# Two-layer paged attention: output products in threes over the next group, and every fourth head transposed by a DMA from ScalarE's queue

## The reference, cut to what matters

```python
x = x + einsum('bct,bcd->bdt', x, weights[subjects])      # x: (32, 32, 512) f32
q, k, v = x @ Wq.T, x @ Wk.T, x @ Wv.T                     # 32 query heads, 8 key heads, D = 128
q, k = rope(rmsnorm(q, q_norm_w), pos), rope(rmsnorm(k, k_norm_w), pos)
k_all = concatenate([k_cache[block_table], k])             # 16 pages of 32 keys, and 32 new keys
v_all = concatenate([v_cache[block_table], v])
scores = where(valid, q @ k_all.T * SCALE, -1e30)          # four query heads share a key head
o = softmax(scores) @ v_all                                # (b, 32, 32 heads * 128)
x = x + o @ Wo.T                                           # (32, 32, 512)
```

## Time and profile before

| | us |
|---|---|
| Median of three runs | 1043.12 |
| Profiled execution, its time | 1038.51 |
| Profiled execution, its span | 1036.7 |
| PE busy (8329 matmuls) | 977.4 (94%) |
| DVE busy | 795.4 (77%) |
| ACT busy | 713.1 (69%) |
| POOL busy | 495.6 (48%) |
| DMA, mean rate over the span | 286 GB/s |

### The profile page before, as it was taken

One profiled execution on the slowest core, in us unless ns is written; L12 is line 12 of the kernel. 1 busy time (PEld: TensorE's weight loads), 2 busy tenths in 40 slices (PEclk: granted clock), 3 DMA queues, 4 the chain that ended last, 5 costly groups with the idle time before them and its releaser, 6 DMA issues.

```text
span 1036.7 us, 24928 instructions
## 1 busy us (share of the span) xinstructions
PE 977.4 (94%) x8329; PEld 775.4 (75%) x8329; DVE 795.4 (77%) x1706; ACT 713.1 (69%) x1943; POOL 495.6 (48%) x642
## 2 busy tenths in 40 slices
PE   3889999999889999899999999999999999999998
PEld 2678888887678788668868857866976986895793
DVE  6789999999997788757857866865875884785680
ACT  4788999988765788647846755764864774675670
POOL 6455666566881266526424623632540641552340
PEclk9999999999999999999999999999999999999999
DMA  5789999989989899768998998997999999899840
GB/s 201 252 303 337 320 384 369 384 279 399 377 289 319 313 329 356 263 186 271 344 252 260 339 266 218 330 299 203 343 295 229 308 317 240 258 359 252 239 147 11
DMA packets 268017, 296.49 MB, mean 286 GB/s; under 512 B 94065, under 2 KB 225649, under 8 KB 265329
## 3 DMA queue, kind: packets, MB, share of 16 engines
q1 hardware_dynamic: 249200, 227.65, 71.7%
q0 software_dynamic: 18688, 67.25, 18.7%
HBM read 231.77 MB, written 46.27 MB: 268 GB/s over the span
## 4 chain that ended last, share of the span: by engine, by line
PE 56%; DVE 14%; SPq 8%; DMA 6%; issue 6%; ACT 6%; POOL 3%; ACTq 0%; DVEq 0%; POOLq 0%
PE ps_o L1410 16%; PE ps_proj L1410 16%; PE ps_o L1488 8%; SPq L641 5%; PE ps_s L1448 4%; PE ps_s L1452 4%; PE ps_t L1459 3%; DMA kt<-k_pages_t 3%; DVE probs L1150 2%; PE ps_rt L1558 2%; DMA vs<-v_pages,v_row 2%; DVE c_stage L1306 1%; PE ps_o L1502 1%; DVE rot L1278 1%; DVE pt L1170 1%
## 5 line engine op out<-in xcount | busy, mean ns | idle before, releaser
L868 POOL TENSOR_SCALAR probs<-probs,recip 128x544 f32<-128x544 f32 (+1 forms) x256 | 158.4, 619 | 376.9 <-DVE recip L1158 373.0
L933 ACT ACTIVATE probs<-probs,neg_max 128x544 f32<-128x544 f32 x256 | 191.3, 747 | 158.2 <-DVE neg_max L1150 157.5
L1150 DVE CUSTOM_DVE_ANT_0 probs<-ps_s,mask,row_scale 128x544 f32<-128x544 f32 x256 | 200.1, 782 | 121.2 <-PE ps_s L1452 118.7
L1488 PE MATMUL ps_o<-pt,vs 128*128 128x128 f16 x3072 | 213.0, 219 | 5.4 <-DVE result L1192 2.5
L1488 PEld LDWEIGHTS ps_o<-pt,vs 128*128 128x128 f16 x3072 | 191.1, 98 | 16.3 <-issue 6.6
L822 POOL TENSOR_TENSOR roped<-rot 128x256 f32<-128x256 f32 x160 | 143.8, 921 | 79.4 <-DVE rot L1270 76.9
L1410 PE MATMUL ps_proj<-wt_hi,x0t_hi 128*128 128x512 f32 x384 | 158.6, 413 | 8.7 <-DVE x0t_lo L1108 7.2
L1410 PE MATMUL ps_o<-wo,ot_hi 128*128 128x512 f16 x512 | 153.5, 382 | 10.0 <-DVE ot_lo L1182 10.0
L1410 PE MATMUL ps_proj<-wt_hi,x0t_lo 128*128 128x512 f32 x384 | 150.7, 392 | 0.0
L1410 PE MATMUL ps_proj<-wt_lo,x0t_hi 128*128 128x512 f32 x384 | 149.8, 390 | 0.0
L856 POOL DMA_INDIRECT vs<-v_pages,v_row x128 | 131.7, 1029 | 22.2 <-issue 19.7
(11 more groups left out here) (145 smaller groups left out, 1590.2 us busy)
## 6 DMA issues: line engine op xcount, KB each, us to landing
kt<-k_pages_t SPq DMA_DIRECT2D x512, 128.0 KB
c_nat<-in_L_cond_k_cache SPq DMA_DIRECT2D x32, 512.0 KB, 5.8
q_t<-stage SPq DMA_DIRECT2D x64, 256.0 KB, 7.5
c_nat<-in_L_cond_v_cache SPq DMA_DIRECT2D x32, 512.0 KB, 7.0
qt<-q_t SPq DMA_DIRECT2D x32, 512.0 KB, 5.6
w_nat<-in_L_cond_Wq SPq DMA_DIRECT2D x8, 1024.0 KB, 8.4
k_pages_t<-c_stage SPq DMA_DIRECT2D x16, 512.0 KB, 5.6
c_nat<-in_L_cond_Wo SPq DMA_DIRECT2D x16, 512.0 KB, 8.1
```

Of the source, the lines that this page charges most:

```text
L868: pool.tensor_scalar(part, part, col(recip, i), 1.0, ALU.mult, ALU.mult).then_inc(p_norm, 1)
L933: act.activation(pr, pr, ACT.Exp, bias=col(neg_max, i), scale=-1.0, accum_out=col(row_sum, i)).then_inc(a_exp, 1)
L1150: dve.tensor_tensor_reduce(out=probs_of(i), in0=ps_s[:, score_cols(i):score_cols(i) + KEYS], in1=mask[(i // HK) % 2][:, mask_at(i):mask_at ...
L1488: ins = pe.matmul(ps_o[n % 2][:, jl * P:(jl + 1) * P], v[:, part, :], pt[i % NPT][:, NCH * half + c, :], start=jl == 0 and c == 0 and k == ...
```

## The change

It has five parts.

1. The projection of a group has a bank of its own, `ps_y`. Its 32 heads of three products each are laid over steps -1 to 28 of the next group, nearly always one head a step (`Y_AT`); for the last group they follow in four steps (`Y_LAST`). `ps_t` has two banks in place of three; up to step 28 `ps_y` serves as the third. `add_residual` runs once per group.
2. So that contexts of the next group can be written while heads of this one are still being read, `ot_hi` and `ot_lo` change their layout from group to group: a head's 128 tokens lie 8 elements apart in even groups and 32 apart in odd ones. ACT and DVE read `ps_o` with a step of 64 or 32 elements to write them. Even groups keep their tokens in another order, which the residual's load and the store undo.
3. From step 52 on each fourth head (i % 4 == 3) is turned by DMA, 51 in all. ACT asks for it, at step i - 1 (`turn_rows`). SP's loop has only keys, queries, new values and results.
4. The new values are weighed in four products over 96 rows in place of eight over 128: `ptn` holds high, low and high again, the last copied by POOL (`tn_copy`). ACT and DVE write `ptn` in two instructions in place of one, and a step earlier. Three DMAs bring a `vn` instead of four, and it needs no zeroes.
5. Wo's late heads are split at two steps in five, up to step 48; one in four on POOL throughout.

```diff
-    vn = [sb(f"vn{i}", [4 * SEQ, HK // 2, 2, 2 * D], F16) for i in range(2)]
+    vn = [sb(f"vn{i}", [3 * SEQ, HK, D], F16) for i in range(2)]
...
-    ptn = [sb(f"ptn{i}", [4 * SEQ, 2, P], F16) for i in range(2)]
-    ot_hi = sb("ot_hi", [P, HQ, GB, SEQ], F16)
-    ot_lo = sb("ot_lo", [P, HQ, GB, SEQ], F16)
+    ptn = [sb(f"ptn{i}", [3 * SEQ, 2, 2, P], F16) for i in range(2)]
+    QUARTER = HQ // GB
+    ot_hi = sb("ot_hi", [P, HQ * GB * SEQ], F16)
+    ot_lo = sb("ot_lo", [P, HQ * GB * SEQ], F16)
     result = [sb(f"result{i}", [P, HID]) for i in range(2)]
     ps_s = psum("ps_s", [P, 3 * CH])
-    NTB = 3
+    NTB = 2
     ps_t = [psum(f"ps_t{i}", [P, CH]) for i in range(NTB)]
     ps_o = [psum(f"ps_o{i}", [P, HPC * P]) for i in range(2)]
+    ps_y = psum("ps_y", [P, HID])
...
-    STEPS = NP2 + 2 * HPC + 3
+    STEPS = NP2 + HPC
     GSTEPS = GB * HK
-    YPARTS = 8
-    YHEADS = HQ // YPARTS
-    YWIN = YPARTS // NHALF
     NBG = GB * NHALF
 
     def at(i, place):
@@ -432,13 +430,12 @@
         n, rest = divmod(i - place, HPC)
         return n if rest == 0 and 0 <= n < NHB else None
 
-    TN, TNE, OE = HPC - 1, HPC, HPC + 2
-    DMA_FIRST, DMA_LAST, STAGED = 2, 11, 3
+    TN, TNE, TNC, OE = HPC - 1, HPC - 1, HPC, HPC + 2
+    DMA_FIRST, STAGED, T_THIRD = 52, 3, 28
 
     def by_dma(i):
 
-        g, r = divmod(i, GSTEPS)
-        return 0 < i < NP2 and g >= 1 and (DMA_FIRST if g > 1 else 8) <= r <= DMA_LAST
+        return DMA_FIRST <= i < NP2 and i % HPC == HPC - 1
...
+    t_banks = [0]
+    for kind, i in tjobs[1:]:
+        t_banks.append((t_banks[-1] + 1) % (3 if (i if kind == "t" else HPC * i + TN) < T_THIRD else NTB))
+
+    def t_bank(kind, i):
+
+        return (*ps_t, ps_y)[t_banks[tjob_no[kind, i]]]
+
+    def held_by(n):
+
+        return max((m for m in range(n) if t_banks[m] == t_banks[n]), default=-1)
+
+    Y_AT = {r: (r + 1,) for r in range(-1, 3)} | {3: (4, 5), 4: (6, 7)} | {r: (r + 3,) for r in range(5, HQ - 3)}
+    Y_LAST = {-1: range(0, 4), 0: range(4, 10), 1: range(10, 16), 2: range(16, HQ)}
+    Y_OUT, Y_OUT_LAST = HQ - 3, 3
...
+    def y_heads(i):
+
+        g = y_group(i)
+        return (Y_AT if g + 1 < NG else Y_LAST).get(i - GSTEPS * (g + 1), ()) if g >= 0 else ()
...
+    def head_at(g, n):
+
+        if g % 2 == 1:
+            return n
+        k, j = divmod(n, QUARTER)
+        return HQ // NHALF * (k // NHALF) + NHALF * j + k % NHALF
+
+    def head_tokens(tile, g, n):
+
+        if g % 2 == 1:
+            return tile[:].rearrange("p (m h) -> p m h", h=HQ)[:, :, n]
+        k, j = divmod(n, QUARTER)
+        return tile[:].rearrange("p (k m j) -> p k m j", k=GB, j=QUARTER)[:, k, :, j]
...
     def late_head(i):
 
-        if i >= LATE_PAIRS:
-            n = WO_EARLY + LATE_PAIRS // 2 + i - LATE_PAIRS
-        else:
-            n = WO_EARLY + i // 2 if i % 2 == 1 else HQ
-        return n if 0 <= i and n < HQ else None
+        k, r = divmod(i, 5)
+        n = WO_EARLY + 2 * k + r // 2
+        return n if i >= 0 and r in (1, 3) and n < HQ else None
 
     def on_pool(n):
-        return n in range(*WO_POOL) and n % 4 == 3
+        return n >= WO_EARLY and n % 4 == 3
...
-        hh = HQ // NHALF
-        return tile[:, hh * h:hh * (h + 1), b % GB, :]
+        g, a = divmod(b, GB)
+        if g % 2 == 1:
+            return tile[:].rearrange("p (a t s h) -> p a s t h", a=GB, t=SEQ, s=NHALF)[:, a, h]
+        return tile[:].rearrange("p (s q a j) -> p s q a j", s=NHALF, a=GB, j=QUARTER)[:, h, :, a]
...
+    def context(n):
+
+        return ps_o[n % 2][:].rearrange("p (h t) -> p t h", t=SEQ if n // NBG % 2 == 1 else NHALF * SEQ)
...
-                for j in range(4):
-                    width = (2 - j // 2) * D
-                    sp.dma_start(vn[s][SEQ * j:SEQ * (j + 1), :, j % 2, 0:width],
-                                 v_new[b].rearrange("t (m j) f -> j t m f", j=2)[j % 2, :, :, 0:width]
-                                 ).then_inc(d_vn[s], 16)
+                for j in range(3):
+                    part = (0, 0, 1)[j]
+                    sp.dma_start(vn[s][SEQ * j:SEQ * (j + 1)], v_new[b][:, :, part * D:(part + 1) * D]).then_inc(d_vn[s], 16)
...
-            def turn_rows(i):
-                sp.wait_ge(v_plo, dma_no(i + 1))
-                sp.wait_ge(t_pv, i - NPT + 1)
-                sp.dma_start_transpose(pt[i % NPT][:], wo[:, HQ + dma_no(i) % STAGED].rearrange("p s f -> p (s f)")
-                                       ).then_inc(d_pt[i % NPT], 16)
-
-            PAGES_IN = {5: 0, 6: 4, 7: 8, 0: 12}
-            for i in range(NP2):
-                if by_dma(i + 2):
-                    turn_rows(i + 2)
-                b, r = divmod(i, HK)
-                n = b + 2 if r >= 5 else b + 1
-                if 2 <= n < B and r in PAGES_IN:
-                    if r == 5:
-                        load_queries(n)
-                    load_pages(n, PAGES_IN[r], NPP // len(PAGES_IN))
-                if r == 2 and 1 <= b < B - 1:
-                    load_new_v(b + 1)
-                    for k in WO_WITH_KEYS.get(b, ()):
-                        load_wo(k)
-                g, a = divmod(b, GB)
-                if r == 3 and a == 2:
+            for b in range(B):
+                if b + 2 < B:
+                    load_queries(b + 2)
+                    load_pages(b + 2, 0, NPP)
+                    load_new_v(b + 2)
+                for k in WO_WITH_KEYS.get(b + 1, ()):
+                    load_wo(k)
+                g, a = divmod(b - GB, GB)
+                if a == 1 and g >= 0:
                     if g >= 1:
                         store_out(g - 1)
                     load_residual(g)
...
+            def tn_copy(n, normed):
+                pool.wait_ge(a_tnhi, n + 1)
+                pool.wait_ge(p_norm, normed)
+                pool.tensor_copy(ptn[n % 2][2 * SEQ:3 * SEQ], ptn[n % 2][0:SEQ]).then_inc(p_tncopy, 1)
+                pool.wait_ge(p_tncopy, n + 1)
 
             norm(0)
             norm(1)
-            for i in range(NP2):
+            for i in range(NP2 + 1):
+                if at(i, TNC) is not None:
+                    tn_copy(at(i, TNC), min(i + 2, NP2))
...
+            def turn_rows(i):
+                act.wait_ge(v_plo, dma_no(i + 1))
+                act.wait_ge(t_pv, i - NPT + 1)
+                act.dma_start_transpose(pt[i % NPT][:], wo[:, HQ + dma_no(i) % STAGED].rearrange("p s f -> p (s f)")
+                                        ).then_inc(d_pt[i % NPT], 16)
...
-                act.activation(ptn[n % 2][0:2 * SEQ].rearrange("p m r -> p (m r)"),
-                               ps_t[tjob_no["tn", n] % NTB][0:2 * SEQ, 0:2 * P], ACT.Copy, scale=P_SCALE
-                               ).then_inc(a_tnhi, 1)
+                for e in range(2):
+                    ins = act.activation(ptn[n % 2][0:SEQ, e], turned_new(n, e), ACT.Copy, scale=P_SCALE)
+                ins.then_inc(a_tnhi, 1)
...
+                if by_dma(i + 1):
+                    turn_rows(i + 1)
...
-                dve.scalar_tensor_tensor(ptn[n % 2][2 * SEQ:4 * SEQ].rearrange("p m r -> p (m r)"),
-                                         ps_t[tjob_no["tn", n] % NTB][0:2 * SEQ, 0:2 * P], P_SCALE,
-                                         ptn[n % 2][0:2 * SEQ].rearrange("p m r -> p (m r)"), ALU.mult, ALU.subtract
-                                         ).then_inc(v_tnlo, 1)
+                for e in range(2):
+                    ins = dve.scalar_tensor_tensor(ptn[n % 2][SEQ:2 * SEQ, e], turned_new(n, e), P_SCALE,
+                                                   ptn[n % 2][0:SEQ, e], ALU.mult, ALU.subtract)
+                ins.then_inc(v_tnlo, 1)
...
-                    g, first = divmod(n, NBG)
-                    if g >= 1 and 1 <= first <= NHALF:
-                        pe.wait_ge(v_res, NHALF * (g - 1) + first)
...
+                pe.wait_ge(p_tncopy, n + 1)
                 pe.wait_ge(v_tnlo, n + 1)
-                for m in range(2):
-                    for e in range(2):
-                        v = vn[b % 2][:, 2 * h + m, e]
-                        jl = 2 * m + e
-                        for part in range(2):
-                            ins = pe.matmul(ps_o[n % 2][:, jl * P:(jl + 1) * P], v[:, part * D:(part + 1) * D],
-                                            ptn[n % 2][:, m, :], start=False, stop=m == 1 and e == 1 and part == 1,
-                                            skip_group_check=True)
+                for jl in range(HPC):
+                    m, e = divmod(jl, 2)
+                    ins = pe.matmul(ps_o[n % 2][:, jl * P:(jl + 1) * P], vn[b % 2][:, HPC * h + jl, :],
+                                    ptn[n % 2][:, e, m, :], start=False, stop=jl == HPC - 1, skip_group_check=True)
...
+            def project_out(g, n):
+                h = head_at(g, n)
                 if g == 0:
-                    wo_done(pe, YHEADS * (k + 1))
-                w, kk = divmod(k, YWIN)
-                w += NHALF * g
```

(24 more changed lines are left out.)

87 lines of the change are left out of this document (39 added, 48 removed).

## The result

The changed kernel takes 1191.2 us (median of 4, 1188.5 to 1196.3) against 1044.05 us before: a ratio of 1.140, interval 1.134 to 1.146. Forecast were 1029 us and a range up to 1052; what came is the rival "transposes land late", with a price of 147 us. The profiled execution took 1190.7 us with a span of 1188.9 us.

The account below looks back on a forecast made before the run. PE was taken as the bound, 79.6 us of an 83.6 us group, the rest waits. Terms -5.8 - 16.2 + 8 + 1.4 - 1.4 = -14.0 us took the median basis of 1043.1 to 1029 us; range 1013 to 1052.

Parts of the forecast that it names:

- transposes land late: Rival, slower: heads turned by DMA land after PE needs them, each microsecond beyond 8.2 costing up to 51 us; 6%.
- need of 8.2 us: Time from ACT asking at step i - 1 to PE reading at step i + 2: some 8.2 us.
- 1.25 us of issue: ACT's time to ask for each DMA with transpose, eight a group; counted as nothing on the sum.
- granted 1.00: TensorE's clock, read as granted in full in both stretches of a group before the change.
- the sum: All terms over the whole kernel: -14.0 us, from the profiled execution's 1038.5 us to 1024.5.
- Two banks: Transposes in steps 28 to 51: 12 us of new waits in place of about 4, so +8 us.
- Projection in threes: Sign of being right: the projection's products in threes all through a group, at 0.65 us a head.
- strided weights: Rival, slower: the projection's strided weight loads cost 392 ns, for 768 products +135 us, about 1164; 6%.
- No wait for keys or values: From step 66 on, keys and values come in time; with the `ot_lo` wait also gone, -16.2 us over six groups.
- ACT as the bound: Rival, slower or same: stepped `ps_o` reads double `ot_hi` and issue holds ACT's queue; 1040 to 1060 us; 6%.
- The DMA engines as the bound: Rival: their 0.99 and 0.97 shares are real work, a group stays near 83 us; 1045 to 1052 us; 10%.

Follow-up runs that it names:

- run 16: The changed kernel with head 8b + 8 turned by DMA in place of 8b + 7, nothing else moved; 1071.8 us.
- run 4: The kernel before the change, with ACT in place of SP asking for its 64 transposes, a step before their head; 1064.6 us against 1039.7.
- run 9: The changed kernel without value gathers after the first two elements, so old values are weighed and output differs from the reference; 1026.4 us.
- run 5: The kernel before the change with part 4 alone (new values in four products); 1049.7 us, ratio 1.0045.
- run 11: The changed kernel with only heads i % 8 == 3 turned by DMA and the new keys' transposes in free columns of `ps_s`; 1046.3 us.
- run 8: As run 1, but with two key pages ahead of the transpose in SP's queue in place of six; 1120.4 us.
- run 12: As run 11, with head 8b + 4 turned by DMA as well; 1080.4 us.
- run 1: The changed kernel with SP asking for the 51 transposes: 8b + 7 behind six key pages, 8b + 3 behind the new values; 1089.2 us.
- run 17: As run 16, with the new keys' transposes in `ps_s` beside the scores; 1073.4 us.
- run 6: As run 1, with every head weighed one step later, so a transpose has more time to land; 1098.8 us.

## Why the prediction was wrong

**The step that failed is the weighing of the rival "transposes land late", at 6%.** It set a need of 8.2 us against a median of 4.2 and a worst of 8.3. Those landings were measured in one queue with the keys and at other moments: in steps 2 to 11 of a group, most of them with a projection part. The change moved each second transposition to 0.4 to 1.2 us behind the last gather, and I looked at where it stands among ACT's instructions, not at what POOL and SP have in flight then. I had costed that step at nothing beyond 1.25 us of issue. Two things came together: the moment (run 16 moves one head by one step, 1191 to 1072) and the room. Spreading the projection took the long steps away that hide late landings (in run 4 up to 14.7 us without a wait), so a late one met PE at once.

**The price of the rival** had the right form. Its chance of 6% rested on no row of the new order. The price said up to 51 us for each microsecond beyond 8.2; 25 heads were late by 4.8 us, 120 us. Missing was the clock, 42 us more: I took the granted 1.00 of the earlier trace rows as given, but here a stall of PE of several microseconds is followed by products at half the rate.

**The rest of the sum stood on the whole.** Run 9 takes only the lateness away and has a span of 1024.6 us, a time of 1026.4, where the sum gave 1024.5 on the profiled execution's basis. That the two agree to 2 us may be partly luck, since the gathers' load is left out too and part 4 gained nothing in run 5. A group takes 79.0 us there (one head's transposition is asked for at 639.76, the same head's of the next group at 718.72) with PE busy for 78.9, where the sum had 78.7 us of work and some 80 in all. With the gathers in place run 11 fits: 1026.4 + 11.4 (26 heads more on PE at 0.44) + 25.9 of waits for `ptn` - 16.1 of waits for banks is 1048 by this estimate, and 1046.3 were measured. Several terms show by themselves:

- Two banks: 12 us of new waits forecast; PE's waits for `pt` of line 1208 are 15.6 us (11.2 + 4.4) over the whole span, 12.9 of them from 350 to 490 us, where these steps lie. Four steps take 446.34 - 433.91 = 12.4 us there; 11.7 + 0.6 was the forecast.
- Projection in threes: 0.66 us for three, 0.65 forecast, so strided weights cost nothing. The load itself takes 149 ns (147 in run 9, at the full clock), not 98, far below the 392 of that rival and under the product's 216. The prediction called 189 ns the slowest load of 128 columns; the trace of before has a few in the first phase that read 224 and 250, so this was a misreading, though no term rested on it. The Trainium skill (Advanced Engine Details and Errata, SBUF Cachelines) states a penalty when each access meets a different line: the trace agrees in direction, by half of the 98 ns, and the product hides it.
- No wait for keys or values is left on PE, and 1.9 us for `ot_lo`; with the gathers out PE is busy for 95% of the span.
- ACT as the bound: `ot_hi` takes 593 ns, and ACT is at 62% (72% in run 9). Not so.
- The DMA engines as the bound: their share is 0.96 at 218 GB/s in the change and 1.00 at 264 GB/s in run 16 (560 to 660 us). The share does not tell it. The Trainium skill (DMA: Bandwidth & Descriptors, Issuing engines are not separate DMA queues) says that other issuing engines only save the time to ask. No run here speaks against it: in SP's queue a transposition lands as late as in ACT's at the same moment (run 8), and through ACT's as early as before at another (run 12). What I drew from it was too much. That the queue adds nothing does not say that the moment of asking costs nothing, and the time to ask is itself not fixed: ACT was held for 4.0 us by one issue in run 4.

**What stays open.** Why a transposition of 1056 small packets is slowed so far beside gathers (67.25 MB / 18688, 3.6 KB a packet) and keys, and the total falls to 135 GB/s, is not shown: whether engines take turns by packet, or something in the transposition itself. Whether ACT's queue adds something of its own at the same moment is not isolated: runs 1 and 4 move queue and moment together. Part 3's effect without part 1 is known only in the old order (run 4). Why run 17's waits for `ptn` did not shrink I didn't follow.

## What to carry over

A transfer that something waits for must be placed by what the other queues have in flight at that moment, on the timeline of all engines that ask for DMAs; its median landing in another place says little. Loops that run several steps apart must be compared in time, not by their step numbers. A transfer that a busy engine asks for also holds what stands behind it on that engine, so its issue time belongs in the sum. And when work is spread evenly, the long steps that hid late landings are gone: list what hid in them first.

## What was not expected of the hardware

- A DMA with transpose of 128 x 1024 values lands after 2.8 to 8.2 us beside key pages alone (run 9), after 9.0 to 17.1 us when it is asked for within 1.2 us behind the last gather (the change), and after 12.6 us there also from SP's own queue (run 8). Moving the gathers or the head by one or two steps changes it by 3 to 5 us.
- With transfers of all three queues in flight (717 to 721 us), the DMA share reads 0.97 to 1.47 and only 135 to 155 GB/s are moved, against 372 four microseconds earlier.
- After a stall of 4.5 us PE's next products run at half rate (1.46 us for twelve against 0.67). The next stall, of 6.9 us, starts 21 us after the first has ended, and the granted clock over the whole stretch is 0.90.
- The issue of a transposition takes up to 5.9 us on SP, between key pages (run 6, median 1.8), and up to 4.0 us on ACT during a burst of them (run 4); the median before was 1.25.
- ACT and DVE read PSUM with a step of 32 or 64 elements within 2% as fast as in a row: 593 and 680 ns against 582 (the page before) and 679.
